# Attention stack of a decoder: Wo and W2 products token-major, the W1 product begun with the high part of X1, packed weights and another opening

## The reference

```python
for i in range(8):
    residual = x
    Q = elu(x @ Wq[i]) + 1; Kf = elu(x @ Wk[i]) + 1; V = x @ Wv[i]     # 16 heads of 64
    KV = sum(Kf * V, over tokens); sumK = sum(Kf, over tokens)
    att = Q * KV * (1 / (Q * sumK + 1e-6))
    x = layer_norm(gelu(att @ Wo[i]) + residual)          # 1024 -> 256
    residual = x
    h = gelu(x @ W1[i])                                   # 256 -> 1024
    x = layer_norm(gelu(h @ W2[i]) + residual)            # 1024 -> 256
```

## Time and profile before

| | |
|---|---|
| median of 3 runs | 3157.49 us (3156.26 to 3159.41) |
| profiled execution, its own time | 3159.65 us |
| its span in the trace | 3158.1 us |
| mean granted clock of TensorE | 0.963 |
| busy in the span: PE, DVE, ACT, POOL | 93%, 74%, 59%, 29% |
| first K, Q, V matmul of the first slots | 20.6 us, then 98.2 us |
| start of one slot, and of those four and eight slots later | 963.1 us, 1276.3 us, 1591.1 us |
| last turn of T in the stack | 2592.0 us |

### The profile page before, as it was taken

One profiled execution on the slowest core, in us unless ns is written; L12 is line 12 of the kernel. 1 busy time (PEld: TensorE's weight loads), 2 busy tenths in 40 slices (PEclk: granted clock), 3 DMA queues, 4 the chain that ended last, 5 costly groups with the idle time before them and its releaser, 6 DMA issues. The chain is left out here.

```text
span 3158.1 us, 35422 instructions
## 1 busy us (share of the span) xinstructions
PE 2933.1 (93%) x11342; PEld 1989.8 (63%) x11343; DVE 2325.5 (74%) x3334; ACT 1862.7 (59%) x2796; POOL 921.5 (29%) x590
## 2 busy tenths in 40 slices
PE   4799999999999999999999999999999977997995
PEld 3566666666666665666566656665666635775563
DVE  7778888888887888887878788879787826763111
ACT  3666676667666776777677767776777713441121
POOL 5004231423152315231513151315131133333002
PEclk8899999999999999999999999999999987996998
DMA  5001101110111001100110011001100008000012
GB/s 129 1 1 23 26 8 32 27 27 6 30 27 27 12 25 27 27 17 19 26 27 17 19 26 27 17 19 26 28 17 4 1 3 269 0 0 24 12 45 77
DMA packets 210193, 92.90 MB, mean 29 GB/s; under 512 B 147056, under 2 KB 203632, under 8 KB 210000
## 3 DMA queue, kind: packets, MB, share of 16 engines
q1 hardware_dynamic: 207360, 83.30, 10.2%
q0 software_dynamic: 2640, 7.21, 0.7%
HBM read 80.24 MB, written 10.22 MB: 29 GB/s over the span
## 5 line engine op out<-in xcount | busy, mean ns | idle before, releaser
L341 PE MATMUL PS<-XTHI,WHI 128*128 128x512 f32 x1536 | 655.5, 427 | 60.8 <-DVE EX L641 41.5
L342 PE MATMUL PS<-XTLO,WHI 128*128 128x512 f32 x1536 | 614.1, 400 | 0.0
L343 PE MATMUL PS<-XTHI,WLO 128*128 128x512 f32 x1536 | 613.6, 399 | 0.0
L269 POOL TENSOR_TENSOR RSTD<-MV,EPS 128x4 f32<-128x4 f32 x68 | 41.1, 605 | 1537.7 <-DVE MV L713 1529.8
L391 PE MATMUL Y<-H,W2S 128*128 128x512 f32 x1024 | 458.2, 596 | 2.7 <-DVE R L703 2.7
L391 PE MATMUL Y<-ATT,WO 128*128 128x512 f32 x1024 | 451.7, 594 | 4.1 <-ACT ATT L540 2.7
L540 ACT ACTIVATE ATT<-INV,CC,CE 128x128 f32<-128x128 f32 x1024 | 424.9, 481 | 3.7 <-DVE INV L687 3.7
L341 PEld LDWEIGHTS PS<-XTHI,WHI 128*128 128x128 f32 x1536 | 294.5, 192 | 153.6 <-issue 64.6
L505 ACT ACTIVATE EX<-PS,BNEG 128x512 f32<-128x512 f32 x256 | 169.8, 686 | 309.9 <-PE PS L343 307.6
L342 PEld LDWEIGHTS PS<-XTLO,WHI 128*128 128x128 f32 x1536 | 294.8, 192 | 83.6 <-issue 20.3
L343 PEld LDWEIGHTS PS<-XTHI,WLO 128*128 128x128 f32 x1536 | 294.0, 191 | 70.0
(11 more groups left out here) (180 smaller groups left out, 4823.9 us busy)
## 6 DMA issues: line engine op xcount, KB each, us to landing
STAGE<-L_attn_Wk SPq DMA_DIRECT2D x128, 64.0 KB, 2.1
STAGE<-L_attn_Wv SPq DMA_DIRECT2D x128, 64.0 KB, 2.1
STAGE<-L_attn_Wq SPq DMA_DIRECT2D x128, 64.0 KB, 2.1
WO<-L_attn_Wo SPq DMA_DIRECT2D x8, 1024.0 KB, 5.5
...
WGU<-L_ffn_r_gate SPq DMA_DIRECT2D x8, 512.0 KB, 10.2
...
```

The lines of the kernel that those rows point to most:

```text
L341: nc.tensor.matmul(out, whi[:, kc, :], xhi[:, kc, :], start=(kc == 0), stop=False)
L342: nc.tensor.matmul(out, whi[:, kc, :], xlo[:, kc, :], start=False, stop=False)
L343: ins = nc.tensor.matmul(out, wlo[:, kc, :], xhi[:, kc, :], start=False, stop=(kc == KD - 1))
```

## The change

Wo and W2 products are made token-major: a block of 128 tokens is stationary, the 256 columns of the weight move, so each 512-column instruction becomes two of 256. The turns of T (`to_tm`) go. The bias is now a row, added by a new DVE instruction (`biased`: T <- Y + bias, 1024 elements), after which ACT applies gelu in place, in one instruction, and DVE adds the residual to T. The product of W1 begins (`hidden_start`) with the high part of X1 for two chunks; the low part comes after, and the turns of X stand between chunks 1 and 2. On DVE the low part X1LO is made between the two instructions of `newton` of pair 2, and the first instruction of `features` is cut in two, K's half ahead of `kf`, Q's half behind. On ACT the gelu for W2 moves behind the gelu of W1's chunk 0. In the opening, DVE starts the attention of tile 0 before it norms tiles 1 to 3, and POOL's first split waits for the norm of tile 0. The host packs the weights, so that a piece is one DMA with whole rows.

```diff
+                    sp.dma_start(STAGE[:, s, :], Wkvq[layer, k, :, :]).then_inc(staged[s], 16)
...
+                    sp.dma_start(STAGE[:, s, 0:2 * KD * P], W1[layer, k - HC, :, :]).then_inc(staged[s], 16)
...
+                sp.dma_start(BA[:, :, cs], bkvq[layer, half, :, :, :]).then_inc(ba_in[half], 16)
...
                 load_wide(WO, Wo, l + 1, wo_in)
-                sp.wait_ge(y_act, g)
-                load_fm(BO, bo, l + 1, bo_in)
+                sp.wait_ge(y_b, g)
+                load_row(BO, bo, l + 1, bo_in)
                 sp.wait_ge(x1, g)
...
@@ -317,10 +306,13 @@
             for k in range(HC):
-                if k % 2 == 0:
-                    t = k // 2
-                    bs = slice(t * TS, (t + 1) * TS)
-                    rstd(RSTD0[:, bs], MV0[:, bs, 1], EPS0, mv0, 2 * t + 2, r0, t + 1)
+                if k == 0 or k == 2:
+                    for t in range(TILES)[:1] if k == 0 else range(1, TILES):
+                        bs = slice(t * TS, (t + 1) * TS)
+                        rstd(RSTD0[:, bs], MV0[:, bs, 1], EPS0, mv0, 2 * t + 2, r0, t + 1)
+                if k == 0:
+                    pool.wait_ge(x0, 1)
                 split_piece(0, k, True)
...
                                                   X[:, t * TS + b, kc * P:(kc + 1) * P], ident[:, :])
                 ins.then_inc(xt_mm, 1)
-            def to_tm(done, value, transposed):
-                pe.wait_ge(done, value)
-                for b in range(TS):
-                    for kc in range(KD):
-                        ins = nc.tensor.transpose(Ytm[:, b, kc * P:(kc + 1) * P], T[:, kc, b * P:(b + 1) * P],
-                                                  ident[:, :])
-                ins.then_inc(transposed, 1)
-            def down(w, src, m, chunks):
-                for c in chunks:
-                    ins = nc.tensor.matmul(Yfm[:, m, :], w[:, c, m * P:(m + 1) * P], src[:, c, :],
-                                           start=(c == 0), stop=(c == HC - 1))
+            def down(w, src, blocks, chunks=range(HC)):
+                for b in blocks:
+                    for c in chunks:
+                        ins = nc.tensor.matmul(Ytm[:, b, :], src[:, c, b * P:(b + 1) * P], w[:, c, :],
+                                               start=(c == 0), stop=(c == HC - 1))
                 return ins
-            def hidden(l, t, g):
+            def hidden_start(l, t, g):
                 if t == 0:
                     pe.wait_ge(w_lo, (l + 1) * PIECES)
                 chunks = (g + 2) * HC if exists(l, t + 1) else LAST * HC
-                for m in range(HC):
+                for m in range(2):
+                    pe.wait_ge(wq, chunks - 1 + m)
+                    for kc in range(KD):
+                        nc.tensor.matmul(PS[:, QB + m, :], W1HI[:, m, kc, :], X1HI[:, kc, :], start=(kc == 0), stop=False)
+                        nc.tensor.matmul(PS[:, QB + m, :], W1LO[:, m, kc, :], X1HI[:, kc, :], start=False, stop=False)
+            def hidden_rest(l, t, g, chunks):
+                last = (g + 2) * HC if exists(l, t + 1) else LAST * HC
+                for m in chunks:
                     if m < 2:
-                        pe.wait_ge(wq, chunks - 1 + m)
-                    elif m < 4:
-                        pe.wait_ge(kv_mul, chunks - 3 + m)
+                        for kc in range(KD):
+                            ins = nc.tensor.matmul(PS[:, QB + m, :], W1HI[:, m, kc, :], X1LO[:, kc, :], start=False,
+                                                   stop=(kc == KD - 1))
+                        ins.then_inc(h_mm, 1)
+                        continue
+                    if m < 4:
+                        pe.wait_ge(kv_mul, last - 3 + m)
                     else:
...
@@ -423,56 +420,54 @@
                 pair(0, 0, 2, 1)
                 if tile:
                     if at_least(l, t, 2):
-                        pe.wait_ge(res2, g - 1)
+                        pe.wait_ge(z_b, g - 1)
...
-                    down(WO, ATT, 0, range(HC - 2))
+                    down(WO, ATT, (0, 2), range(HC - 2))
                     pe.wait_ge(att, g * PAIRS + 4)
-                    down(WO, ATT, 0, range(HC - 2, HC))
+                    down(WO, ATT, (0, 2), range(HC - 2, HC))
                 pair(1, 0, 2, 1)
                 if tile:
-                    down(WO, ATT, 1, range(HC)).then_inc(y_mm, 1)
-                pair(2, 0, 2)
-                if tile:
-                    to_tm(y_act, g + 1, yt_mm)
-                pair(2, 1)
+                    down(WO, ATT, (1, 3)).then_inc(y_mm, 1)
+                pair(2, 0, 2, 1)
...
-                        pe.wait_ge(res1, g + 1)
+                        pe.wait_ge(y_b, g + 1)
...
-                    down(W2S, H, 0, range(HC))
+                    down(W2S, H, (0, 1))
                 pair(3, 0, 2, 1)
                 if before:
-                    ins = down(W2S, H, 1, range(HC - 3 if tile else HC))
+                    down(W2S, H, (2,))
+                    ins = down(W2S, H, (3,), range(4 if tile else HC))
-                    if more:
-                        pe.wait_ge(kf, (g + 2) * HC)
                     for kc in range(KD):
+                        if more:
+                            pe.wait_ge(kf, (g + 2) * HC - 1 + kc)
...
-                        ins = down(W2S, H, 1, range(HC - 3, HC))
+                        ins = down(W2S, H, (3,), range(4, HC))
...
                     pe.wait_ge(x1_hi, g + 1)
+                    hidden_start(tl, tt, g)
                     pe.wait_ge(x1_lo, g + 1)
+                    hidden_rest(tl, tt, g, range(0, 2))
...
-                    hidden(tl, tt, g)
-                if before:
-                    to_tm(z_act, g, zt_mm)
+                    hidden_rest(tl, tt, g, range(2, HC))
...
+            def gelu_down(biased, done, value):
+                act.wait_ge(biased, value)
+                nc.scalar.activation(T[:, :, :], T[:, :, :], ACT.Gelu_apprx_tanh).then_inc(done, 1)
...
                     nc.scalar.activation(H[:, m, :], PS[:, QB + m % 4, :], ACT.Gelu_apprx_tanh,
                                          bias=B1[:, m:m + 1]).then_inc(h_act, 1)
+                    if m == 0 and before:
+                        gelu_down(z_b, z_act, g)
                     if between is not None:
                         weigh(*between, (m,))
...
-                    zl, zt = slot_of(l, t - 1)
-                    gelu_down(z_mm, B2, b2_in, z_act, zl, zt, g)
+                if before and not tile:
+                    gelu_down(z_b, z_act, g)
                 if exists(l, t + 2):
                     input_hi(g + 2)
                 if tile:
...
+                nc.vector.tensor_scalar(EX[:, b, 2:4, :], EX[:, b, 2:4, :], -1.0, 1.0, ALU.add, ALU.add).then_inc(snap, 1)
                 if t == 0 and b == 0:
                     dve.wait_ge(b_neg, 2 * l + (p // 2 + 1))
-                dve.wait_ge(snap, n + 1)
+                dve.wait_ge(snap, 2 * n + 1)
                 for i in range(2):
                     c = 2 * p + i
                     nc.vector.scalar_tensor_tensor(EX[:, b, 2 + i, :], PS[:, KB + i, :], BUP[:, 0, c:c + 1],
                                                    EX[:, b, 2 + i, :], ALU.add, ALU.max).then_inc(kf, 1)
+                nc.vector.tensor_scalar(EX[:, b, 4:6, :], EX[:, b, 4:6, :], -1.0, 1.0, ALU.add, ALU.add).then_inc(snap, 1)
+                dve.wait_ge(snap, 2 * n + 2)
                 for i in range(2):
                     c = 2 * p + i
                     nc.vector.scalar_tensor_tensor(EX[:, b, 4 + i, :], PS[:, QB + i, :], BUP[:, 2, c:c + 1],
                                                    EX[:, b, 4 + i, :], ALU.add, ALU.max).then_inc(wq, 1)
...
@@ -656,6 +650,8 @@
                                                    EX[:, b, 2 + i, :], ALU.add, ALU.mult).then_inc(kv_mul, 1)
                 if normed1 is not None:
                     normed(*normed1)
+                if biased2 is not None:
...
+            def newton(l, t, p, between=None):
                 n, b = (l * TILES + t) * PAIRS + p, p % 2
                 dve.wait_ge(inv, n + 1)
                 nc.vector.tensor_tensor(EX[:, b, 4:6, :], EX[:, b, 4:6, :], INV[:, b, :, :], ALU.mult).then_inc(residue, 1)
+                if between is not None:
+                    hidden_lo(between)
                 dve.wait_ge(residue, n + 1)
                 nc.vector.scalar_tensor_tensor(INV[:, b, :, :], EX[:, b, 4:6, :], 2.0, INV[:, b, :, :], ALU.subtract,
                                                ALU.mult).then_inc(recip, 1)
...
+            def biased(mm, value, bias, bias_in, layer, t, free, done):
+                if t == 0:
+                    dve.wait_ge(bias_in, (layer + 1) * 16)
+                if free is not None:
+                    dve.wait_ge(*free)
                 dve.wait_ge(mm, value)
-                nc.vector.tensor_tensor(R[:, w, :, :], Ytm[:, :, :], add, ALU.add).then_inc(res, 1)
```

(35 more changed lines are left out.)

95 lines of the change are left out of this document (42 added, 53 removed).

## The result

The changed kernel takes 3185.93 us (median of 4 runs, 3180.56 to 3189.39), the kernel before 3158.2: a ratio of 1.0089, 95% interval 1.0073 to 1.0105. It is slower by 28 us, 0.9%. The profiled execution of the change has a span of 3183.2, 25.1 more than that of before.

What follows compares the result with a forecast made beforehand. PE bounded ordinary slots (75.9 us); after the change a ring of waits through PE, ACT and DVE (76.9) would. Seven layers +37, three ordinary slots +3, opening -6.5: +33.5 on 3157.5 gives 3191, range 3128 to 3230.

Steps and rivals of the forecast that it cites:

- Turns of T, Wo and W2: PE's work: two sets of turns go, -1.76 a slot; 256-column instructions at 0.216 add 0.16; PE alone 74.3.
- the exposed weight loads: Rival for Wo and W2: 64 more loads a slot at 0.175 are not overlapped, +359, 3516; chance 0.02.
- Turns of X behind two chunks: In W1, PE waits for ACT's gelu at two chunks, twice 0.5 lost; PE's slot 75.3.
- The ring: Waits through PE, ACT and DVE, K of pair 3 to the next: 76.9; PE waits 1.6 for `kf` of pair 2.
- Ordinary slots: Slots without eight splits: each loses 1.0 against 75.9; over a layer 76.9, 76.9 and 78.6.
- half pitch: Rival: after each slot's new wait PE runs at 1.2 instead of 2.4 GHz, 1.5 more a slot: 3237, chance 0.06.
- the likeliest case: The forecast itself: whole kernel 3191, own range 3165 to 3228, chance 0.58.
- Split slots: Slots where POOL's split pieces hold DVE back: the eight-split slot 86.9, a layer 319.3, +5.3 a layer.
- Sum against trace: Layer cost: new addition 319.3 minus the trace's 314.0, +5.3, though the same addition gave 312.3 for before.
- The opening: Before the first layers: PE starts at 17.2 instead of 20.6, pair 0 sooner on DVE; -6.5 taken, bounds 0 to 15.
- At nothing: Packed weight DMAs were given no gain, since no engine waits for a piece inside the stack's loop.
- The ring is shorter than PE: Rival: `kf` of pair 2 comes before PE asks, slot 75.3, in all 3132; chance 0.20.

Runs made afterwards that it cites:

- both: Changed kernel with the bias of Y ahead of the reduction of pair 1 and ACT's gelu table load ahead of XTHI: 3076.1 us, 0.9731 of before.
- y_early: Changed kernel with DVE's bias of Y moved ahead of the reduction of pair 1: ratio to before 0.9854, -74 us to the changed kernel.
- y_late: Changed kernel with DVE's bias of Y moved behind the denominators of pair 1: ratio to before 1.0354, +84 us to the changed kernel.
- whole_snap: Changed kernel with the first instruction of features whole again, not cut in halves: ratio to before 0.9969, -38 us to the changed kernel.
- table_early: Changed kernel with ACT's gelu table load put ahead of XTHI: ratio to before 0.9943, -46 us to the changed kernel.
- turns_sooner: Changed kernel with PE's turns of X between the high and low parts of W1's two chunks: ratio to before 0.9989, -32 us to the changed kernel.
- unrolled: Changed kernel with the loop over layers written out on all five engines: ratio to before 1.0065, -8 us to the changed kernel.
- open_old: Changed kernel with the old opening on DVE and POOL put back: ratio to before 1.0078, -0.1% to the changed kernel.

## Why the prediction was right

It was right in sign and in its mechanism: a ring of waits longer than PE's work, with PE waiting for `kf` of pair 2. That the number came so close, 3191 against 3186, is luck. Not all of its steps were right, and the errors cancel.

*Turns of T, Wo and W2.* 0.216 an instruction is what rows show, and the exposed weight loads did not come. PE's own slot is 73.4 and not 74.3. Most of the 0.9 is in a place that the sum had no term for: in `both` the groups of 36 matmuls for a pair take 8.24 to 8.44, before 8.45 to 8.85, 1.3 less in all. Wo's and W2's groups and the smaller turns of T (0.79 a set, not 0.88) give 0.3 of it back. Behind a W2 or Wo instruction of 512 columns the second matmul started 0.63 after the first; behind one of 256 columns it is 0.42.

*Turns of X behind two chunks.* "Twice 0.5 are lost": 0.5 and 0.42.

*The ring.* The forecast of 76.9 with PE waiting 1.6 for `kf` of pair 2 named the wait, its place and its cause. The wait is 2.3 in slot 12, 3.2 in slot 13 and 1.9 in slot 14, start to start. That the bias behind the reduction lengthens the ring (y_early, y_late) and that the cut instruction does (whole_snap) is shown by runs that change nothing else. That ACT's later end does follows from table_early and turns_sooner by way of the wait that did not grow.

*Ordinary slots* are mis-sized: on average over slots 4 to 27, 77.8 behind the slot with eight splits, 80.2 in the one with W1's splits, 78.9 at the loop's end, where the forecast had 76.9, 78.6 and 76.9. Two things were missing, half pitch and the loop's end. Slots 4, 12 and 29:

```profile
325.90:403.10 77.20, 74.49 (x338) 61.81 (x337) 64.96 (x98) 52.54 (x81) 12.68 (x8) 1.00 0.09 30
963.70:1042.20 78.50, 75.75 (x337) 62.95 (x336) 65.47 (x103) 52.68 (x81) 12.95 (x10) 0.98 0.09 29
2322.40:2400.40 78.00, 74.43 (x337) 61.71 (x336) 67.18 (x97) 51.80 (x77) 23.27 (x16) 1.00 0.06 19
```

Slots 4 and 12 do the same work with the same wait for `kf` (2.14 and 2.17); the clock fell in slot 12 alone, and it is 1.4 longer (78.53 and 77.15). Where the clock stayed at 1.00 and no loop ends, the forecast holds to 0.6: slots 4, 8, 24 and 28 last 77.1 to 77.2, slot 29, with W1's splits, 78.0, and slot 14 of `unrolled` 76.7. Half pitch is in 14 of the 24 slots, 4.6 a layer, against 1.8 before. The rival had it at 0.06 and the likeliest case left it out, because the earlier trace rows followed a wait of 2.3 and the expected ones were 1.6; the waits were longer, and half pitch itself makes the ring longer. The loop's end is the second part: 1.6 to 3.4 against 0.7 to 1.1.

*Split slots.* 86.9 was too long: 82.9 on average (85.2 before). PE waits at other places there. In slot 15 it waited for 2.3 at K of pair 2, 1.5 at the turns of R and 2.8 at the turns of X before; now it waits 2.1 at K of pair 3, 2.2 at the turns of R and 0.3 for X1LO. The addition had kept more of the old waits. Taken together: the three other slots were to lose 3.6 and lost 8.1, this one was to lose 1.7 and gained 2.3, which makes 5.8 where 5.3 was said.

*Sum against trace.* The forecast set its new sum, 319.3, against the 314.0 of the trace. The same addition gives 312.3 for the kernel before, so sum against sum is +7.0 a layer, which would have made 3203. The measured +5.9 lies between.

*The opening.* -6.5 was taken, and open_old against the changed kernel shows -6.5 at slot 3. The slots before the layers gained 4.2 more, which the sum left out.

*At nothing.* From slot 31 on 5.2 were gained that the sum had as zero. 3.7 of it lie in the last slots of the stack; the other 1.5 are within what that stretch varies by in the variants. And the packed weights are not worth nothing.

*The rivals.* "The ring is shorter than PE" would have been right with one DVE instruction 2.3 us earlier: y_early is 3112, below the 3132 it gave.
